# Attention passes of a graph kernel: the fourth slot's gathered rows are added by VectorE, not by an identity product on TensorE

## What is computed

```python
xl = (x @ Wl).reshape(n, H, C)
xr = (x @ Wr).reshape(n, H, C)
e = jax.nn.leaky_relu(xl[src] + xr[dst], NEG_SLOPE)
score = jnp.einsum('ehc,hc->eh', e, att)
smax = jax.ops.segment_max(score, dst, num_segments=n)
ex = jnp.exp(score - smax[dst])
denom = jax.ops.segment_sum(ex, dst, num_segments=n)
alpha = ex / jnp.maximum(denom[dst], 1e-16)
out = jax.ops.segment_sum(alpha[:, :, None] * xl[src], dst, num_segments=n)
```

## Time and profile before

| what | value |
|---|---|
| median of 3 runs | 2531.91 us (2526.62 to 2535.03) |
| the profiled execution, its own time | 2526.24 us |
| its span, first to last instruction | 2524.4 us |
| busy over the span: PE, DVE, ACT, POOL | 79%, 66%, 54%, 60% |
| mean granted TensorE clock | 0.912 of 2.4 GHz |

### The profile page before, as it was taken

How to read it: one execution, slowest core, us unless ns; L and a number is a source line. 1 busy time by engine, 2 the same in 40 slices (tenths; PEclk the granted TensorE clock), 3 DMA queues, 4 the chain that set the end, 5 groups by cost and what they waited for, 6 DMA issues and landing times. The chain is left out here.

```text
span 2524.4 us, 37785 instructions
## 1 busy us (share of the span) xinstructions
PE 1983.8 (79%) x8650; PEld 1357.8 (54%) x8650; DVE 1668.5 (66%) x3532; ACT 1364.3 (54%) x5328; POOL 1519.3 (60%) x1740
## 2 busy tenths in 40 slices
PE   0665666566399989599999999958489999999975
PEld 0443444444277776356666666634256666666644
DVE  9534333333266667388888888866278888888866
ACT  0355555555300003177777877764157877777773
POOL 3377777777600008877766666619877666666602
PEclk9777777877699999899999999988799999999997
DMA  3387575655498962355555555621255555555532
GB/s 97 81 192 169 169 168 173 165 167 168 117 267 265 270 191 71 101 158 155 149 146 158 147 144 146 134 66 39 72 155 154 148 144 149 146 144 149 139 89 96
DMA packets 272019, 369.89 MB, mean 147 GB/s; under 512 B 40436, under 2 KB 230902, under 8 KB 271831
## 3 DMA queue, kind: packets, MB, share of 16 engines
q1 hardware_dynamic: 207159, 195.75, 28.0%
q0 software_dynamic: 64512, 171.82, 24.9%
q10 hardware_dynamic: 160, 0.20, 0.0%
HBM read 272.59 MB, written 101.50 MB: 148 GB/s over the span
## 5 line engine op out<-in xcount | busy, mean ns | idle before, releaser
L1132 POOL DMA_INDIRECT gath<-gather_table,SRCI x880 | 840.2, 955 | 351.0 <-issue 245.1
L1343 ACT ACTIVATE gath<-gath 128x32 f32<-128x32 f32 x3520 | 766.3, 306 | 0.0
L1178 PE MATMUL p_sums<-gath,OH 128*128 128x272 f32 x1760 | 473.4, 408 | 67.5 <-issue 25.2
L733 POOL DMA_INDIRECT rows_by_src<-gath,node x440 | 438.5, 997 | 137.7 <-issue 116.5
L1146 PE MATMUL p_expd<-gath,ident 128*128 128x512 f32 x880 | 425.3, 606 | 65.5 <-DMA gath<-gather_table,SRCI 65.0
L667 PE MATMUL p_expd<-X,HOTS 128*128 x880 | 302.5, 505 | 219.8 <-DVE HOTS L626 215.8
L1178 PEld LDWEIGHTS p_sums<-gath,OH 128*128 128x128 f32 x1760 | 318.9, 193 | 173.4 <-issue 75.9
L667 PEld LDWEIGHTS p_expd<-X,HOTS 128*128 128x128 f32 x880 | 210.8, 250 | 300.6 <-issue 264.0
L1206 DVE SCALAR_TENSOR_TENSOR work<-p_expd,VEC 128x512 f32<-128x512 f32 x440 | 283.1, 685 | 115.6 <-PE p_expd L1151 109.0
L1151 PEld LDWEIGHTS p_expd<-node,LBC 128*128 128x128 bf16 x2640 | 258.6, 98 | 152.1 <-issue 127.1
L1151 PE MATMUL p_expd<-node,LBC 128*128 x2640 | 324.3, 273 | 0.0
(11 more groups left out here) (285 smaller groups left out, 2251.7 us busy)
## 6 DMA issues: line engine op xcount, KB each, us to landing
gath<-rows_by_src SPq DMA_DIRECT2D x122, 514.0 KB
LBC<-hots_by_node SPq DMA_DIRECT2D x220, 128.0 KB
HOTS<-hots_by_edge SPq DMA_DIRECT2D x220, 128.0 KB, 2.4
LBC<-local_rows SPq DMA_DIRECT2D x110, 128.0 KB
hots_by_node<-gath SPq DMA_DIRECT2D x110, 128.0 KB
hots_by_edge<-gath SPq DMA_DIRECT2D x110, 128.0 KB, 2.9
gath<-gather_table,SRCI POOLq DMA_INDIRECT x880, 3.0
rows_by_src<-gath,node POOLq DMA_INDIRECT x440
```

The lines of the kernel that those rows point to most:

```text
L733: pool.indirect_dma_start(sup_d[:, :], bass.IndirectOffsetOnAxis(POSI[:, i:i + 1], 0), U[:, q % 4, g, :], None, bounds_check=EP - 1, oob_i ...
L1132: pool.indirect_dma_start(ROWS[:, i % (RING * G), 0:XW], None, tab_d[:, :], bass.IndirectOffsetOnAxis(SRCI[:, i:i + 1], 0)).then_inc(gathe ...
L1178: ins = pe.matmul(sums[k][:, 0:RW], OH[:, a % 2, g, :], slots(a, g, g + 1)[:, 0, :], start=(g % 2 == 0), stop=(g % 2 == 1))
L1343: ins = act.activation(R[:, h * C:(h + 1) * C], R[:, h * C:(h + 1) * C], ACT.Copy, scale=R[:, D + h:D + h + 1])
```

## The change

The identity products now cover slots 0, 1 and 2 of a group. The fourth slot's columns of `expd` hold only the destination rows (its first bf16 product starts the columns afresh), and DVE's product(q) adds the gathered rows of that slot first, into T, and then takes max and slopes in three instructions instead of two. A semaphore, `plus`, orders the add before the last of them.

```diff
-                            for k in range(2):
-                                pe.matmul(expd[q % 2][:, k, :].rearrange("p (g n) -> p g n", g=2), ident[:, :], slots(q, 2 * k, 2 * k + 2)[:, :, 0:D],
-                                          start=True, stop=False)
+                            pe.matmul(expd[q % 2][:, 0, :].rearrange("p (g n) -> p g n", g=2), ident[:, :], slots(q, 0, 2)[:, :, 0:D],
+                                      start=True, stop=False)
+                            pe.matmul(expd[q % 2][:, 1, 0:D], ident[:, :], slots(q, 2, 3)[:, 0, 0:D], start=True, stop=False)
...
-                                                    PARTS3[:, bass.ds(tiles[g // 2], 1), c, :], start=False, stop=(g % 2 == 1 and c == 2))
+                                                    PARTS3[:, bass.ds(tiles[g // 2], 1), c, :], start=(g == G - 1 and c == 0), stop=(g >= 1 and c == 2))
...
+                            SLOPES = VEC[:, 2, :].rearrange("p (h c) -> p h c", h=H)
+                            LAST = Tv[:, q % 2, G - 1, :, 0:C]
                             dve.wait_ge(expanded, q + 1)
-                            for k in range(2):
-                                ins = dve.scalar_tensor_tensor(Tv[:, q % 2, 2 * k:2 * k + 2, :, 0:C].rearrange("p g h c -> p g h c"),
-                                                               expd[q % 2][:, k, :].rearrange("p (g h c) -> p g h c", g=2, h=H), 0.0,
-                                                               VEC[:, 2, :].rearrange("p (h c) -> p h c", h=H).unsqueeze(1).broadcast_to([P, 2, H, C]),
-                                                               ALU.max, ALU.mult)
-                            ins.then_inc(weighted, 1)
+                            dve.tensor_tensor(LAST, expd[q % 2][:, 1, D:2 * D].rearrange("p (h c) -> p h c", h=H),
+                                              slots(q, G - 1, G)[:, 0, 0:D].rearrange("p (h c) -> p h c", h=H), ALU.add).then_inc(plus, 1)
+                            dve.scalar_tensor_tensor(Tv[:, q % 2, 0:2, :, 0:C], expd[q % 2][:, 0, :].rearrange("p (g h c) -> p g h c", g=2, h=H), 0.0,
+                                                     SLOPES.unsqueeze(1).broadcast_to([P, 2, H, C]), ALU.max, ALU.mult)
+                            dve.scalar_tensor_tensor(Tv[:, q % 2, 2, :, 0:C], expd[q % 2][:, 1, 0:D].rearrange("p (h c) -> p h c", h=H), 0.0,
+                                                     SLOPES, ALU.max, ALU.mult)
+                            dve.wait_ge(plus, q + 1)
+                            dve.scalar_tensor_tensor(LAST, LAST, 0.0, SLOPES, ALU.max, ALU.mult).then_inc(weighted, 1)
```

More of the change, by code:

```diff
@@ L1042, in build @@
                 gathered = [sem(f"gathered{k}") for k in range(RING)]
-                expanded, lin_ready, weighted, scored = (
-                    sem("expanded"), sem("lin_ready"), sem("weighted"), sem("scored"))
+                expanded, lin_ready, plus, weighted, scored = (
+                    sem("expanded"), sem("lin_ready"), sem("plus"), sem("weighted"), sem("scored"))
                 by_row, ends_ready, in_rows, carried, copied, grow_ready = (
```

## The result

| what | before | changed |
|---|---|---|
| median | 2533.47 us (4 runs, 2526.62 to 2536.26) | 2498.09 us (4 runs, 2494.84 to 2501.62) |
| profiled execution | 2526.24 us | 2494.84 us |
| span | 2524.4 us | 2493.0 us |

The ratio is 0.9865, 95% interval 0.984 to 0.989: 1.35% faster, 34 us by this ratio and 35 us between the two medians. The forecast was 36 us and 2496 us, with a range of 2482 to 2520 us.

The account below looks back on a forecast made before the run. The prediction took a ring of waits through ACT, PE and DVE as the bound: per chunk -0.84 + 0.40 - 0.26 = -0.70 us, times 51 is 36 us, so 2531.9 - 36 = 2496 us, range 2482 to 2520.

Parts of the forecast that it names:

- PE's term: On PE, the second identity product has 256 columns instead of 512: 0.43 us less per expansion.
- DVE's term: In DVE's product, four instructions before the reduce instead of two: d = 0.40 us more per group, 1.72 against 1.32.
- The wait on `plus`: In DVE's product, costed at nothing; a rival had it cost 0.21 us without overlap, 39 us slower, chance 0.07.
- The case of no overlap: Rival: DVE's neighbouring instructions do not overlap, d = 0.69 us, 4 us gained, no change, 2528 us; chance 0.08.
- The ring: Waits of ACT, PE, then DVE set the time of a chunk (four groups): 22.19 us before, 0.70 us less forecast.
- The wait at the product of step 0: DVE's wait for PE's expansion in a chunk's first step: from 1.34 us down to some 0.2.
- that before ends: DVE's wait in step 0 for PE's transpose of the scores: from 0.66 us down to 0.3.
- none at carry and shift: DVE's waits at carry (0.33 us) and at shift (0.18 us) were to disappear.
- PE idle before the sums of step 2: PE's wait for ACT's weighing, 0.36 and 0.52 us before, was to be 0.8 us or more.
- The reading of carry's "issue": DVE's 0.33 us wait at carry, listed only as "issue", was taken as a wait for PE's transposes.
- The count: Over both layers, 51 chunks times 0.70 us each: 36 us gained.
- The rival of the clock: More idle time lowers PE's clock to 1.2 GHz for a tenth of the chunks: 110 us slower at most; chance 0.03.

Follow-up runs that it names:

- g3: Only the PE half of the change, fourth slot's gathered rows left out, against the kernel before: 2477.58 us against 2536.9, ratio 0.978.
- g4: Only the DVE half of the change, fourth slot's gathered rows counted twice, against the kernel before: 2544.97 us against 2536.9, ratio 1.0038.
- f1: The same kernel as g3 on another chip, where the kernel before took 3052 us: ratio 0.997 to it.
- g1: DVE adds two, one, one, no slots in steps 0 to 3, in place in PSUM; against the kernel before: 2477.56 us against 2538.71, ratio 0.977.
- g2: The changed kernel with a second add in every product, against the kernel before: 2546.7 us against 2533.6, ratio 1.0049.
- e and f: Two series of four variants (halves, doubled add, other placements) on two chips, against the kernel before: ratios 0.991 to 1.007 and 0.992 to 1.014.
- e1 to f4: The eight runs of e and f, four on each chip, against the kernel before at 3039 and 3052 us: ratios 0.991 to 1.014.

## Why the prediction was right

- **PE's term**, 0.43 us an expansion: 3.02 became 2.60 us.
- **DVE's term**, d = 0.40: 0.39 us. The wait on `plus` costs nothing that these rows show: L1214 starts 0.33 us behind L1211, as far as L1209 starts behind the add of the same size. The case of no overlap (0.69 in the prediction; its own rows add up to 0.68) is excluded by these rows: neighbours overlap by 0.08 to 0.09 us (1211.67 + 0.68 against 1212.27). The Trainium skill's page "VectorE: DVE Perf Modes", section "The DRAIN you can't avoid", says that the next operation does not start until the pipeline is empty, but also, which the prediction left out, that one that is not held starts earlier. The rows above agree with the second sentence and not with the first.
- **The ring**: -0.70 us a chunk was forecast, -0.72 measured. The wait at the product of step 0 was to be some 0.2 us and is 0.31, that before ends 0.3 and is 0.26, none at carry and shift. One sign of the forecast failed: PE idle before the sums of step 2 was to be 0.8 us or more and is 0.68. The prediction looked at PE's wait for the weighing in step 3 only, and missed those of steps 0 and 1; what PE saves is spent there in part (the sums of step 1 start 0.02 us before the shift, 1216.59 against 1216.61, where it was 0.12, 1215.45 against 1215.57). It costs nothing, since in step 2 PE waits for ACT in any case. The reading of carry's "issue" as PE's transposes is borne out: with PE's expansion shorter it is gone (the change, g3), with DVE's part alone it stays at 0.34 (g4).
- **The count**, 51 x 0.70 = 36 us, is right in size, and partly by luck to the microsecond. In the profiles the stretch from the first sums to the last expansion shrank from 562.4 to 544.1 us in the first layer and from 563.9 to 544.3 in the second, 37.9 us in all. The two ends of the passes gave 3.9 back: from the last expansion to the last sums it takes 38.8 and 40.1 us instead of 37.9 and 37.2, part of it at the lower clock. The fills (the steps of a pass before its first sums) are even: 42.2 for 39.7 us in the first layer, 39.4 for 41.7 in the second. Outside the passes the changed execution is another 2.4 us longer, so that the two spans differ by 31.4 us. That the medians differ by 35 owes something to these small terms, which the forecast did not have. (The second pass of the kernel before ends at 2456.7 us, later than the 2440 given above.)
- **The rival of the clock** came true in part, in the fills and at next to no price. These are the windows of the two fills in the kernel before, the changed one, g3 (PE's half, so the shorter expansion too) and g4 (DVE's half, the full expansion), with the columns of f1's windows:

```profile
1048.00:1088.00 40.00, 29.07 (x137) 16.48 (x138) 23.20 (x36) 8.39 (x31) 30.25 (x33) 0.96 0.57 152
1812.00:1854.00 42.00, 30.59 (x137) 17.18 (x138) 23.44 (x36) 8.95 (x34) 31.76 (x34) 0.91 0.55 150
```

```profile
1051.00:1093.00 42.00, 30.71 (x137) 19.13 (x137) 25.51 (x51) 8.50 (x32) 31.65 (x35) 0.80 0.55 149
1799.00:1838.00 39.00, 28.31 (x136) 17.62 (x136) 25.54 (x50) 8.41 (x31) 29.56 (x32) 0.88 0.56 150
```

```profile
1057.00:1097.00 40.00, 29.31 (x136) 18.11 (x135) 22.81 (x35) 8.16 (x30) 30.25 (x33) 0.84 0.57 148
1793.00:1834.00 41.00, 30.44 (x137) 18.93 (x138) 23.14 (x36) 8.80 (x33) 30.95 (x34) 0.83 0.56 151
```

```profile
1055.00:1094.00 39.00, 28.40 (x136) 15.75 (x135) 24.99 (x49) 7.94 (x30) 29.55 (x32) 0.96 0.56 148
1825.00:1867.00 42.00, 31.95 (x137) 17.41 (x137) 25.45 (x51) 8.66 (x33) 31.95 (x34) 0.87 0.56 149
```

In the first fill the clock is 0.96 in both kernels with the full expansion and 0.80 and 0.84 in the two with the shorter one (0.83 in g1 and g2, which have it too); in the second layer's fill it is below 1.00 in all four, and they are closer, 0.91 and 0.87 against 0.88 and 0.83. That speaks for the shorter expansion as the cause in the first fill, from one profile of each kernel; it is not shown. The changed kernel's first fill takes 2.5 us more and its second 2.3 us less. In the chunks the clock stayed at 1.00, though PE is idle three times in each:

```profile
1100.00:1300.00 200.00, 15.51 (x37) 1.00 0.56 155
```

(This is the window of L1207, the add: us, DVE busy, clock, DMA share, GB/s.)

## What to carry to other kernels

Where engines wait for one another in turn, work has no price of its own: follow the ring hop by hop and ask of each place what waits behind it. Moving 0.43 us from one engine to another that needs 0.39 for it gained 0.72 us a chunk, though the two amounts all but cancel, and choosing the places (two slots where DVE was waiting for PE, none where PE was waiting for ACT), with a cheaper form of the add, gained 1.2. Measure each half alone before adding up: the halves of this change add up to 51 us and gain 35 together.

## What was not expected of the hardware

- The same kernel before took 2533 to 2539 us in the runs of the result and on the three chips of g1 to g4, and 3039 and 3052 us on the two of e and f. In the profiled executions of e1 to f4 the mean granted clock was 0.82 to 0.85 against 0.91, and whole chunks took 21 to 32 us. The edits under test move a chunk by 1 us and drown in it; a comparison needs a chip whose beat is steady.
- A 128x256 fp32 product after a 128x512 one takes half its time, 0.22 us a record against 0.43 (two records from 1207.79 to 1208.22, and from 1206.93 to 1207.79), though its weights take 0.19 us to load (the mean of L1147's loads on the profile's page): the loads do not show in the spacing of the records.
